# New written-out orders for five engines and new PSUM places in an attention-and-FFN block kernel

## The reference, cut to what matters

```python
def attention(x):
    qkv = x @ qkv_w.T + qkv_b                    # 3 x 16 heads x 16 channels
    q, k = apply_rope(q, cos, sin), apply_rope(k, cos, sin)
    scores = einsum('bhid,bhjd->bhij', q, k) * scale
    scores = where(causal, -inf, scores)
    out = einsum('bhij,bhjd->bhid', softmax(scores), v)
    return out @ proj_w.T + proj_b

def ffn(x):
    H = gelu(x @ U1 @ V1 + b1)
    return H @ U2 @ V2 + b2

x = x + layernorm(attention(layernorm(x)))
return x + layernorm(ffn(layernorm(x)))
```

## Time and profile before

| what | value |
|---|---|
| median of 3 runs | 1230.49 us (1224.57, 1230.49, 1235.24) |
| the profiled execution | 1225.88 us |
| its span, first to last instruction | 1224.1 us |
| mean granted TensorE clock | 0.984 |
| busy: PE, DVE, ACT, POOL | 1165.3, 939.7, 940.3, 661.9 us |

### The profile page before, as it was taken

The page is one execution under the profiler, slowest core; times in us unless marked ns, Lnnn a source line. Parts: engine busy times, 40 slices in busy tenths (PEclk is TensorE's granted clock), DMA queues, the critical chain, the costliest instruction groups (busy, mean ns, idle before and its releaser), DMA issues.

```text
span 1224.1 us, 25832 instructions
## 1 busy us (share of the span) xinstructions
PE 1165.3 (95%) x9843; PEld 620.4 (51%) x9843; DVE 939.7 (77%) x1452; ACT 940.3 (77%) x1898; POOL 661.9 (54%) x724
## 2 busy tenths in 40 slices
PE   5789999999999999999999999999999999999995
PEld 3544446554564456545654565455545444455452
DVE  7788887788878886789678958886778886467665
ACT  4356877688868887787779876987688689678794
POOL 5065513873397339833884378438833443247466
PEclk9789999999999999999999999999999999999997
DMA  5665644547446753684357537672464743403312
GB/s 169 205 98 128 142 68 78 145 114 140 97 111 135 115 118 111 131 141 105 93 157 106 118 87 175 103 142 81 118 125 89 138 97 104 145 11 118 116 69 103
DMA packets 99259, 142.22 MB, mean 116 GB/s; under 512 B 24896, under 2 KB 60992, under 8 KB 99136
## 3 DMA queue, kind: packets, MB, share of 16 engines
q1 hardware_dynamic: 99136, 140.58, 51.5%
HBM read 79.70 MB, written 51.38 MB: 107 GB/s over the span
## 4 chain that ended last, share of the span: by engine, by line
PE 57%; POOL 11%; DMA 9%; SPq 8%; DVE 6%; ACT 6%; issue 2%; POOLq 0%; ACTq 0%; DVEq 0%
PE PV L853 14%; PE RING L835 11%; PE RING L800 9%; PE RING L905 5%; PE RING L898 4%; PE RING L755 3%; ACT PB L1170 3%; DMA QK<-split_parts 3%; SPq L612 3%; DVE MB L986 3%; PE RING L767 3%; SPq L628 2%; POOL EO L541 2%; POOL TB L538 2%; PE RING L864 2%
## 5 line engine op out<-in xcount | busy, mean ns | idle before, releaser
L1170 ACT ACTIVATE PB<-RING 128x512 f32<-128x512 f32 (+2 forms) x1280 | 624.0, 567 | 154.3 <-PE RING L835 141.0
L986 DVE TENSOR_REDUCE MB<-RING 128x2 f32<-128x1024 f32 (+2 forms) x448 | 497.7, 1143 | 107.2 <-PE RING L806 56.9
L835 PE MATMUL RING<-QK 64*128 64x512 f32 (+3 forms) x1536 | 317.3, 395 | 6.9 <-DMA QK<-NSROW 4.2
L1261 POOL TENSOR_SCALAR_AFFINE_SELECT PB<-PB 128x512 f32<-128x512 f32 x256 | 161.1, 639 | 293.7 <-ACT PB L1170 293.2
L800 PE MATMUL RING<-QK 62*128 62x512 f32 (+3 forms) x1536 | 292.3, 390 | 11.8 <-DMA QK<-split_parts 7.2
L835 PEld LDWEIGHTS RING<-QK 64*128 64x128 f32 x1536 | 167.3, 187 | 164.3 <-ACT PB L1170 95.5
L986 DVE TENSOR_REDUCE M<-RING 128x2 f32<-128x768 f32 (+1 forms) x186 | 190.9, 1041 | 60.1 <-PE RING L806 59.2
L853 PE MATMUL PV<-PB,VL 128*32 128x512 f32 (+3 forms) x2048 | 224.5, 523 | 2.1 <-POOL PB L1261 1.2
L800 PEld LDWEIGHTS RING<-QK 62*128 62x128 f32 x1536 | 152.5, 187 | 131.7 <-DVE MB L986 38.7
L806 PE MATMUL RING<-MASKK,MASKQ 64*128 64x128 bf16 (+1 forms) x768 | 108.0, 247 | 0.0
L1195 ACT ACTIVATE F_H<-RING,F_B 128x512 f32<-128x512 f32 x128 | 80.7, 694 | 23.4 <-PE RING L898 23.2
(11 more groups left out here) (125 smaller groups left out, 1502.8 us busy)
## 6 DMA issues: line engine op xcount, KB each, us to landing
QK<-split_parts SPq DMA_DIRECT2D x372, 128.0 KB, 5.7
split_parts<-PARTS SPq DMA_DIRECT2D x60, 256.0 KB, 3.1
split_parts<-EO SPq DMA_DIRECT2D x60, 256.0 KB, 3.6
ATT<-OT SPq DMA_DIRECT2D x128, 64.0 KB
INV<-inverse_sums SPq DMA_DIRECT2D x32, 256.0 KB
block_mid<-Y SPq DMA_DIRECT2D x16, 512.0 KB, 4.9
F_X<-block_mid SPq DMA_DIRECT2D x16, 512.0 KB, 5.0
out<-F_Y SPq DMA_DIRECT2D x32, 256.0 KB, 2.1
```

Source lines behind the costliest of these rows:

```text
L835: ins = e.matmul(m[:, i, :], QK[g % 3][r, 1, k, 128 * j:128 * j + 128], QK[g % 3][r, 0, k, 512 * c + off:512 * c + 512], start=True, stop= ...
L986: e.tensor_reduce(acc, ring(("max", g, s, u), pairs, n), AX.X, ALU.max).then_inc(v_max, 1)
L1170: e.activation(buf[:, h, pairs[0]:pairs[-1] + 1, :], strip(("score", g, s, u), pairs, n), ACT.Exp).then_inc(a_exp, 1)
L1261: e.affine_select(buf[:, :, 0:128], buf[:, :, 0:128], pattern=[[0, 4], [1, 128]], base=0, channel_multiplier=-1, compare_op=ALU.is_ge, fil ...
```

## The change

Only `ORDERS` and `PLACES` are replaced, by strings from a new search in which transfers are a queue that each leaves behind its predecessor. The steps are the same, except that PE has two `warm` more (4 matmuls of zeros in place of 2). Taking the fewest steps that have to move to get from the old order to the new one, 365 of PE's 2812 steps move, 236 of ACT's 1863, 174 of DVE's 1057, 106 of POOL's 528 and 51 of SP's 270; hardly one moves further than 20 places. The bank differs for 1048 of 2243 PE steps. The first 11 steps of SP and its last 21 stay as they are.

Moves that the text below speaks of, read from the strings:

- POOL, opening: `ones(1)` and `ones(2)` stood 2nd and 3rd; now `ones(1)` stands behind `ln_pow(1, 1)`, and `ones(2)` behind `rope(1, 0, 1, 1)`, just ahead of `select(0, 0)`. `rest(1, 0, 0)`, which stood behind `select(0, 3)`, now stands ahead of `select(0, 2)`.
- DVE, opening: `xt_low(1, 1, 0)` goes from ahead of `chain_low(0)` to behind it.
- PE, opening: `product(0, 1)` and `product(0, 2)` now stand directly ahead of `score(0, 4, 0)`; `product(0, 2)` stood behind it.
- PE, group 25: `qk(7, 1, 3, 0)` took the bank that `qk_out(7, 1, 2)` empties; now it takes the one that the `exp` of `score(25, 5, 2)` empties, and `product(25, 2)` stands directly ahead of it. ACT now does that `exp` and the next ahead of `qk_out(7, 1, 2)`.
- SP: `att_spread(0, 1)` goes ahead of `send(2, 0, 0)`, and `att_spread(6, 0)` ahead of `att_load(27, 1)`. In the same way `att_spread(1, 1)`, `(2, 1)` and `(5, 1)` go ahead of the next `shift`, `att_spread(5, 0)` ahead of `load_group(26)`, `att_spread(7, 1)` ahead of loads for the feed-forward part.
- SP: `load_group(10)`, `(18)`, `(22)` and `(26)` now stand behind two to five short steps that they stood ahead of, one of them an `att_sums` each time. Eleven `att_load` and eight `store` change sides with a `shift` or `load_group`.
- POOL: `select(30, 10)` goes ahead of `f_pow(1)`. `select(5, 0)` and `select(5, 1)` now stand behind `att_scale(0, 1, 1)` and `rest(2, 0, 1)`, which stood between the two.
- POOL as a whole: adding up the lengths of what stands ahead of each of the 256 `select`, 66 have over 0.7 us more of POOL's other work ahead of them than before, and 39 have over 0.7 us less.

The diff, cut to the first line of four engines and to SP's:

```diff
     "PE": (
-        "hxxqqqqqqqqvhvvvxxfqqqqqvqqvqvvxxmmvmmmmqFqqqvmmmqqmsmqmssmqmssmmvmssvmssmxmxmsmtpmpmmsmsmssspsmssmqssmmss"
+        "HxxqqqqqvqqqhvvvxxfqqqqqvqqvvHvxxhmmqmmmmqvFqqvqmmqmmmsqsmqmsmvmssmsmmvmssxxmsmsstmmpmmmsmppsmsspsmssmmms"
...
     "ACT": (
-        "llllxxqlqqqrlllxxrvqlllqqqlxrvrvxFvqqveqeleeeqlleleevexlexetreeleeeeeeeeeeoeereeeeeeeqeteeqleeeeeeeeeeeqeee"
+        "llllxxlqqqqlllrxxrvvqqqqllrllxrvxqFvllqqelveqeleeerveeextexeeeeeeeeoeeeeeeeereeeeeleteqqeeeeleeeeqeeeeele"
...
     "DVE": (
-        "ssssdsqssxxsdwssssdrrrrrlrxxlfsrsrrrsrlrxsldsxsssmdmsmmsmmXmmmmmmmmmmmmmmxambmxmmmmmmmmmmmmmmmmmmmmammbmm"
+        "ssssdsqsxxssdwssssrrrrrlrxxldsrrrrrlrfxslssxdmmmmssmsmsdsXsmmmmmmmmmmmmmmambxmmxmmmmmmmmmmmmmmmmmmmmammbsm"
...
     "POOL": (
-        "pooppprrrsprsrssrllsrsssrrssslsrrrlssssssssssssssssssssspsssrararslrsrsrsaslassrsrrrlrrslssssPsssPssRRsssR"
+        "pppporrrrrosslpssrlsrsssrrssslsrrlsssssssssssssssssssspssssrrraalrrsssrsaalsssrrsrrrrllsPsssssssRPssssRss"
...
     "SP": (
-        "ssxgssgHghgsashgsahsagahagaamhgoambohsbgsahsasagaahgxaatmhgatobmohbassghssaagaahgaxtamhobamgohbsstaghssaag"
-        "aathgaxamhobagtmohsbasghassagaahgaxamhoabgmohtbsstaghssaagaahagxatamhogabmhotsbgsahssaaghaagaamhoabtmgobhtg"
-        "aahaLahaIaamotbamoRbtSSSSNSSSStNSSSStNSSSSSSSSSSSSSSSSSSSS"
+        "ssxgssgHghgasshgashsagaahgaamhgoamobhbsgsahssaagaahgxahtamamotbgobhassghssaagaahgxtaahmaombgotbhassghssaag"
+        "aahgxahtamaobtmghobsasghassagaahgxatahmtoambghosbsaghssaagaahgxaamthobatmgobhsagshssaaghaagaamhoabtmgobhta"
+        "gahaLaahIaatmtobamobRSNSSSSSSSStNtSSSNSSSSSSSSSSSSSSSSSSSS"
...
```

More of the change, by code:

```diff
@@ new lines @@
+        "smspmsmsspmsssmppsmsspssmssspmmsmpssmssstsmpsssmpssmsspmssppmssssvmmvvvmssmxpsmsssxmsssspppmmssqqqmssmpssm"
+        "qmssmqqssssssvvvvmmqqssmtpmssmjpssssmjjjssmmppssmssxpmssxppmssssqqqqmmspssmppmssmqqmssmqqssssmjjssmpmssmsp"
+        "tssssmjjssssmpssmpsssmmsppssmsspmsmssppmssspmsssspmsspmsssmpmsspmsssmpsssmmpsssssmpmstsmmsspmmsspmsssmssms"
+        "psmsspsmssmspsmsmsspssmppmmssspsmmssspsmssmsptssmsspsmsmsspsmmssspssmppmssmvvmmsspmssvvmssssxpssmssppxssss"
+        "mpqmssssqqqmssmqqssmppmmssqqvmssmvvvssmmtjjjssssmjpmmssxpssmsspxsmsssppmmmqqqqqmsssspssmmqsspmmssqqssssmpj"
@@ new lines @@
+        "mmssjpssssmtppmssmpmssmpsssmjmssjsmmssspssmsspsmssppmssssspmssmspssmppssmsssspsmsssspssmpmssmsmstmssmpmmss"
+        "pmsssmspmsmssppssmssmmsspssmpmsssmppmssssspmsmsspsmssmpssssmtpsmssmspssmsspmssmppssmvssmmvvvssmmxsspssssmp"
+        "ppssmmxsspmmssqqssssmqqssssmpmmssqvvqqqssmvvmssmtpjjssssmjjpmsssmpxmsssspppxmssmpssssqmmsqqqmssmqqmsmqqsss"
+        "smpppssmjmssmjssssmpmssmtpssmsmjmssmpjmssmpssssspsmmsspsmsspsspmmssspssmssspmmssppssmpssmsspsmsmsssssppsms"
+        "tsmsmpmssmpssmsmsspsmsmsssmpsssmpmsmsspmsssppmssmpssmmsssmspssmsspsssssmtpsmssmpsmssmpssmppmmssvvmssmvvssm"
@@ new lines @@
+        "eeeeeeeeeoeeeeeeeeyeeeoeeeeeeeeeeeeeeeteeeeeyeeeeeeeeeeeeeeoyeeyeeeeeeoeeyeeeeeeeeeeteeeeeeeeeeeyeyeeoeeve"
+        "eeeeeeeeeveeeeeeeeeeoeeeeeeeeeteeeeeeeyeeeeoeeeeeeeeyeeeeeeeeeoeeyeeeeeeeeeyteyeyyyeeeeeeeeeeeoeeeeeeeeeeo"
+        "eeeeeeeeeeeeeeteeeeeeTeeeTeeeeeeeeeoeeTeeeeeoeeeeeeeTeeeeeeeeeeeeeeeeeTggggTgogggggggTggTggTggQTggggggTgTg"
+        "gggTggggggTgggygggggTgQgTgngnngnTyggggTgggngTggTQggggyynggggnTnggTggnggTQggggTgygnyynggnyggggTggQggTgngTgg"
+        "TgggggTgggnggnTggggQTnnTgnggngggnggggggnggQngnnggggggngQnnnnn"
@@ L217 @@
[L217 to L220 removed]
+        "pppporrrrrosslpssrlsrsssrrssslrsrrlsssssssssssssssssssspssssrrraalrrsssrsaalsssrrsrrrrllsPsssssssRPssssRss"
@@ L255 @@
+        "6401562314562301423563012563401256342501253412503450125346012453601235640123564012563421056120356012356012"
+        "34562103412560123456120356034121562012035641235640312541203434012312012034121203412012343401212034120000"
 )
```

150 lines of the change are left out of this document (68 added, 82 removed).

## The result

| | runs | median, us | lowest to highest |
|---|---|---|---|
| before | 11 | 1230.07 | 1224.28 to 1235.24 |
| after | 11 | 1219.34 | 1214.54 to 1229.28 |

The changed kernel takes 0.9913 of the time before, 95% interval 0.9891 to 0.9936: 10.7 us less. That is inside the range, and twice the 5.2 us of the forecast. In a second series of runs it was 0.9931 (0.9909 to 0.9953).

What follows compares the result with a forecast made beforehand. PE was taken as the bound from 84 to 1206 us; -0.5 - 1.2 - 1.5 - 1.2 - 0.8 = -5.2 us from 1230.5 gave 1225.3 us (chance 0.42), range 1209 to 1240, the forecast's own 1219 to 1232.

Steps and rivals of the forecast that it cites:

- The sum: Whole kernel: gains of 0.5, 1.2, 1.5, 1.2 and 0.8 us add to -5.2 us, carried to the median: 1225.3 us.
- The named stops: PE's stops at product(5, 1), qk(7, 1, 3, 0), proj(6, 0, 0), product(30, 10): gains 1.2, 1.5, 1.2, 0.8 us.
- waits for loads that the forecast put at 0: Four load_group behind two to five steps: between 0 and 18 us, taken as 0 since loads arrive with time to spare.
- a new wait for QK above 1 us in the middle: Sign against the forecast: it is wrong if new waits for QK above 1 us stand in the middle.
- The opening: First 84 us: shifted maxima land earlier, select(0, 2) ends at about 83.1, PE goes on 0.3 us sooner: -0.5 us.
- falls once near 83: Sign for the opening: PE's clock still falls once near 83 us.
- 0, within 1 us either way: Feed-forward part and tail: PE busy throughout, same work, last steps keep their order but for POOL's powers: no change.
- Steps moved ahead of shift: cost 0: SP's queue: one or two steps of 0.4 to 2.4 us fit into its 6.1 us waits for chain_low: cost 0.
- POOL's waits for INV: Sign at POOL: its waits for the spread inverses fall from 17.5 us to below 8.
- Hidden waits: First rival: a tenth of the weight loads' 95.5 + 38.7 us also goes, 13.4 us more: 1211.9 us; chance 0.24.
- It doesn't do what it says: Second rival: transfers were hidden anyway, half of 3.3 us of direct waits goes: 1228.9 us; chance 0.18.
- Late selects: Slower rival: POOL's selects come late, 27 more pieces cost 9.1 us, in all +6.4: 1236.9 us; chance 0.16.

Runs made afterwards that it cites:

- the control: The kernel before, unchanged, run as if it were a new one: 0.9999 (0.9974 to 1.0024) of before, 12 runs.
- The runs with and without zeros: Kernel before with only SP's new order in the middle: 1.0409 of before; the same with 102 matmuls of zeros in three long PE stops: 1.0343.
- The five moves: Kernel before with only att_spread(0, 1), att_spread(6, 0), select(30, 10), qk(7, 1, 3, 0) with its exp, and ln_stats(3, 0, 0) moved: 0.9944, 6.9 us faster.

## Why the prediction was right, and where its sizes were off

**The sum.** It went against one execution, 1225.88 us, and the difference "in us" was carried over to the median. This step failed in size. That execution had none of the clock's falls that five other profiles of the old middle have, and less idle time than four of them, so what the change removes was undervalued. That the measured 10.7 us lie inside the range is partly luck: terms that the sum didn't have, the clock in the middle and the loss in the feed-forward part, go against each other.

**The named stops.** They were right in place and nearly in size. Means over six old and four new profiles:

| stop of PE | forecast gain | old, new, us | gain |
|---|---|---|---|
| `product(5, 1)` | 1.2 | 1.02, 0 | 1.0 |
| `qk(7, 1, 3, 0)`, then `score(25, 6, 0)` | 1.5 | 2.78, 0.84 | 1.9 |
| `proj(6, 0, 0)` | 1.2 | 1.75, 0 | 1.7 |
| `product(30, 10)` | 0.8 | 0.56, 0 | 0.6 |

(0: none over 0.25 us.) 5.2 us against 4.7. As forecast, the wait at the bank of `qk_out(7, 1, 2)` moved to a later bank rather than went.

**What the sum left out.** `chain_turn(8)`, 1.55 us in the mean of the old profiles, and `product(20, 3)`, 0.91 us, neither in the new ones. Against these the new middle has waits for loads that the forecast put at 0: 1.17 us at `max(16, 0, 0)` in the first profile, 2.04 us at `max(22, 0, 0)` in that of the kernel with the old feed-forward part. By the prediction's own sign, a new wait for QK above 1 us in the middle, it would be wrong. But the sign can't tell the kernels apart: four of the six old profiles have such waits too (1.42 us in the control), and the one that the prediction read is not among them. All open waits of `max` for loads in the middle add up to 2.5 us in the mean of the old profiles and to 4.2 in the new ones: a loss of 1.8 us.

**The opening.** The runs can't tell -0.5 us from nothing (1.0001, 0.9972 to 1.0029). The profiles speak for a little more: `product(0, 11)` ended at 115.6 us in the mean of the four with the new opening (114.0 to 117.5) and at 117.9 in the ten with the old one (117.2 to 118.4). The working was not right: `select(0, 2)` ended at 84.3 (forecast 83.1), and though the stop of 2.16 us shrank to 0.34, the `score` behind it began at 86.8 us in the first profile instead of 83.4, not 0.3 us sooner. That the clock "falls once near 83" was wrong: in both profiles of the changed kernel it falls elsewhere, for 17.1 us in all against 23.9 us before.

**The clock.** It is the term that the prediction didn't have for the middle: 3.3 of its 12.0 us by the estimate above. The Trainium skill, "TensorE: Matmul & The Clock Gate", "HAM oscillation — how this bites in real kernels", tells that idle gaps in PE's work bring the lower clock back. The runs with and without zeros agree with it: 0.58 and 1.00 behind the same stop.

**The feed-forward part.** "0, within 1 us either way" failed: 3.2 us lost by the profiles, 5.2 by the runs. The prediction looked at the order of POOL's powers and not at what runs beside DVE. The Trainium skill states the rule in "SBUF — State Buffer", section "Who interferes with whom": an operation of DVE in a mode with two ports and one of GpSimd exclude each other, and whichever comes second waits for the whole of the first. The trace agrees in the lengths, 5.23 us for four operations beside four of POOL and 1.37 without; which mode DVE was in it doesn't show.

**SP.** "Steps moved ahead of shift: cost 0" held; SP's own wait for `chain_low` even grew from 177.5 to 225.4 us without harm. POOL's waits for INV, forecast to fall below 8 us, rose to 31.1 while both stops behind them went: a wrong sign to look for, since that wait costs something only where PE needs what stands behind it in POOL's queue.

**The rivals.** Hidden waits: the time came half-way to its 1211.9 us, but not through its mechanism; 95.5 + 38.7 us became 95.1 + 36.4. "It doesn't do what it says": no, 10.7 us instead of 1.6. Late selects: no; `product` waited 10.4 us for them, less than the 13.2 of the earlier trace rows. Whether transfers can overtake one another, which the second rival needed, no run tested: in the one stop that was followed to SP it mattered when a transfer was issued (204.31 or 220.74).

**What stays open.** The five moves give 6.9 of the middle's 12.9 us. They bring the idle time down, but in their one profile leave the middle 6 us longer than the new one's mean: 1.4 us of it is idle time, some 2 us half clock (6.8 us of it against 2.6), and for the rest, short waits inside PE's busy time, no single move was found. Nor was it settled how much of the run-by-run spread the opening's clock causes.

## What to carry to other kernels

A profile is one execution: before a sum of small stops is priced, profile the same kernel again, and price each stop by its mean and by the clock behind it, not by the luckiest run. Follow a stop through every engine that it names until something outside the orders (a load, a store, a port) ends the chain; the dearest one that the prediction missed, at `chain_turn(8)`, was a load that DVE's row hid. And take orders of several engines as one plan: with SP's part alone this middle was 50 us slower, with all of it 13 us faster, and the part that was worth leaving away, the feed-forward part, was left away for all engines at once.

## What was not expected of the hardware

The clock's fall is not the same from run to run at the same stop: 2.74 us at `qk(7, 1, 3, 0)` in the first profile had none behind it, 2.44 us in the control had 3.4 us at half clock, 3.64 us with the new feed-forward part 6.8 us. Over the changed kernel's 11 runs the span grew by 0.53 us for each us at half clock, from 1212.8 to 1227.5, with the same program.

Four operations of DVE of 0.34 us each took 1.3 us each when POOL worked beside them, while POOL's own took 1.28 to 1.34 us, against a median of 1.28 us: here nearly the whole price fell on DVE. It is not always so: in the control one of POOL's `f_res` that began beside the last operation of `f_rows(12)` took 1.45 us.
